# One product with the scalar features instead of two in the message pass of a four-layer graph network

## The chip, the cores and the metric

The kernel runs on one core of one Trainium2 chip. The metric is the device time of one execution in microseconds (us). Of the kernel before, three runs took 8483.14, 8487.90 and 8493.29 us; the median is 8487.9 us. A difference of about 0.2% (17 us) is what such runs can tell from none.

The engines have these names in the profile: PE is TensorE (matrix products), PEld its weight loads, DVE is VectorE, ACT is ScalarE, POOL is GpSimd (it issues the gathers), SP issues the plain DMAs. PSUM is the memory that PE writes; it has eight banks of 512 float32 per partition, `c.ps[:, bank, :]`.

## What is computed

The kernel computes four graph layers one after the other on 6250 nodes and 100,000 edges. The change is in the first, whose messages are, for each edge:

```python
h = jax.nn.silu(edge_scalars @ (fc_w1 / ...)) * SILU_NORM
w = h @ (fc_w2 / ...)
w0, w1, w2, w3 = the four quarters of w, 32 wide each
se = s[edge_src]          # 32 scalar features of the source node
ve = v[edge_src]          # 32 x 3 vector features
es = edge_attr[:, :1]
ev = edge_attr[:, 1:4]
mid_s0 = w0 * se * es
mid_s1 = w3 * jnp.einsum('eui,ei->eu', ve, ev) / SQRT3
mid_v0 = (w1 * se)[:, :, None] * ev[:, None, :]
mid_v1 = (w2 * es)[:, :, None] * ve
mid_scal = jnp.concatenate([mid_s0, mid_s1], axis=1)
mid_vec = jnp.concatenate([mid_v0, mid_v1], axis=1)
ns = jax.ops.segment_sum(mid_scal, edge_dst, num_segments=N) * inv
nv = jax.ops.segment_sum(mid_vec, edge_dst, num_segments=N) * inv
out_s = ns @ (w_lin2_s / fan)
```

So two of the four products have the scalar features `se` as a factor: one row of 32 with `w0`, three rows with `w1` times the three components of `ev`.

## The kernel before

The function `messages` holds this pass. The edges are sorted by destination and lie 128 to a chunk. There are 784 chunks, in 98 groups of 8 (`G8`, index `q`); a group has two halves of 4 chunks (`b` is 0 or 1). A ring of 4 groups (`RING`) holds gathered rows and loaded weights. Each engine has its own program; they meet at semaphores only, so what is written first on an engine runs first on it.

- **SP** (L930 to 962) loads the weights and attributes of a group (`s.pay4`, called `fld` in the trace), and stores finished rows.
- **POOL** (`gather`, L1149) issues one indirect DMA a chunk, which fetches the source rows of 128 edges into `rows`. It waits for the indices (ACT, L970) and, from the fifth group on, until the products of the group four places back are done (`m.prod`).
- **ACT** (`scaled`, L976 to 997) lays the weights of a half in PSUM, in banks 4 and 5 for `b` = 0 and 6 and 7 for `b` = 1. Two instructions copy `w0` and `w2` of the four chunks (L985), twelve copy `w1` and `w3` times one component of `ev` each (L989). It starts on a half when the products of the half two places back are done. In bank 4 lie the twelve rows of `w1`, then the four rows of `w0`; in bank 5 the same of `w3` and `w2`. Between halves it does steps of the node layer that runs behind (L1387 to L1407).
- **DVE** (L1016 to 1106) makes the one-hot places of a group (`hot`, L813 through `one_hot`), the products in five steps (`products`, L1031 to 1072), and adds what PE returns to `acc` (`add_item`, L824). The five steps are: 0, `w3` times the vector features into `s.dot`, which the trace calls `u` (L1056); 1, `w0` times the scalar features (L1060); 2, the three rows of `w1` times the scalar features (L1063); 3, `w2` times the vector features (L1067); 4, the sum of `s.dot` over the three components (L1071), with which `m.prod` is signalled.
- **PE** (L1103 to 1124) multiplies the one-hot places of a chunk with its products (L1118, 257 columns) into PSUM bank 0 or 1. It waits at each half for `m.prod`, and at each chunk until the sum two places back has been added (`ahead = 2`).

The order on DVE is written out in `reduce` (L1082 to 1099): step 0 of half 1; then for the four chunks of half 0 an add and a step each; then `hot` of the next group and step 0 of its half 0; then for the chunks of half 1 an add and a step of the next group's half 0 each. A step of the node layer (L1417 to L1430), or the add of the rows left over in a node tile (L857), stands in between in some groups.

The names: `plain_in` and `scaled_in` are the parts of the PSUM banks with the unscaled and the scaled weights, `s.prod4` is the output seen as chunk, four rows, 64 columns. `s.lin2` are the weights by which the summed messages are multiplied afterwards; their rows follow the column order of `prod4`.

Of the kernel before, what the change touches and what calls it, by code (L numbers as in the profile page):

```python
# [18 lines left out]
ALU = mybir.AluOpType  # L19
ACT = mybir.ActivationFunctionType  # L20
# [889 lines left out]
def messages(c, s, table, layer):  # L910
# [9 lines left out]
    rows_of = lambda r: ring_rows(c, r, D)  # L920
    ahead = 2
    bank = lambda q, j: item(q * G8 + j) % ahead
    scaled_in = lambda b, t, j: c.ps[:, 4 + 2 * b:6 + 2 * b, (j % 4) * 3 * MUL:(j % 4 + 1) * 3 * MUL] if t is None else \
        c.ps[:, 4 + 2 * b + t, 0:4 * 3 * MUL].rearrange("p (j a u) -> p j a u", j=4, a=3)
    plain_in = lambda b: c.ps[:, 4 + 2 * b:6 + 2 * b, 4 * 3 * MUL:4 * 4 * MUL].rearrange("p t (j u) -> p t j u", j=4)

    with nc.Block() as block:

# [36 lines left out]
        @block.scalar  # L965
        def _(act):
            def indices(i, r):
                q = RING * i + r
                act.wait_ge(m.pay[r].sem, i * 16 + (m.pay[r].n + 16))
                nc.scalar.activation(c.idx["dst"][:, at(q, G8, 0, G8)], s.pay4[:, r, :, SRC],  # L970
                                     ACT.Copy).then_inc(c.idx_ready.sem, 1)
                nc.scalar.activation(c.lo["dst"][:, at(q, G8, 0, G8)], s.pay4[:, r, :, LO],
                                     ACT.Copy).then_inc(m.kept.sem, 1)

            def scaled(i, r):
                q = RING * i + r  # L976

                act.wait_ge(m.pay[r].sem, i * 16 + (m.pay[r].n + 16))
                for j in range(G8):
                    if j % 4 == 0 and q:  # L980
                        act.wait_ge(m.prod.sem, m.prod.n + q * 2 + j // 4 - 1)
                    if j % 4 == 0:
                        w02 = s.pay4[:, r, j:j + 4, 0:P].rearrange("p j (t u) -> p t j u", t=4)[:, 0:4:2, :, :]
                        for t in range(2):
                            nc.scalar.activation(plain_in(j // 4)[:, t, :, :], w02[:, t, :, :], ACT.Copy)  # L985
                    w13 = s.pay4[:, r, j, 0:P].rearrange("p (t u) -> p t u", t=4)[:, 1:4:2, :]
                    for a in range(3):
                        to = scaled_in(j // 4, None, j)[:, :, a * MUL:(a + 1) * MUL]
                        last = nc.scalar.activation(to, w13, ACT.Copy,  # L989
                                                    scale=s.pay4[:, r, j, EV + a:EV + a + 1])  # L990
                    if j % 4 == 3:
                        last.then_inc(m.scaled.sem, 1)
                    if j == 3 and after(i, r, 3, RING):
                        indices(*after(i, r, 3, RING))
                    layer.act(act, q * G8 + j)
            lay_places(c, nc.scalar)
            indices(0, 0)
            indices(0, 1)
            indices(0, 2)
            written_out(NG, scaled, RING)  # L1000
            for t in range(NCH, NCH + layer.after):
                layer.act(act, t)
# [15 lines left out]
        def _(dve):  # L1018
# [14 lines left out]
            def products(i, r, b, step):  # L1033


                q = RING * i + r
                js = slice(4 * b, 4 * b + 4)
                w = plain_in(b)
                g = rows_of(r)[:, js, :].rearrange("p j (t u) -> p j t u", t=4)
                if step == 0:  # L1040
                    if b == 0:
                        dve.wait_ge(c.gathered[r].sem, i * (16 * G8) + (c.gathered[r].n + 16 * G8))
                    if q:

                        dve.wait_ge(c.mm.sem, c.mm.n + done(q * G8 + 4 * b - 4))
                        h = 2 * (q - 1) + b
                        if h < STASH:
                            sent = c.stashed[h % (2 * RING)]
                            dve.wait_ge(sent.sem, sent.n + 16 * (h // (2 * RING) + 1))

                    dve.wait_ge(m.scaled.sem, q * 2 + (m.scaled.n + b + 1))
                    if not (first(q) and b == 0):

                        dve.wait_ge(m.prod.sem, q * 2 + (m.prod.n + b))

                    nc.vector.tensor_tensor(s.dot, scaled_in(b, 1, 0), g[:, :, 1:4, :],  # L1056
                                            ALU.mult).then_inc(m.dotted.sem, 1)
                elif step == 1:

                    nc.vector.tensor_tensor(s.prod4[:, js, 0, MUL:2 * MUL], w[:, 0, :, :], g[:, :, 0, :], ALU.mult)  # L1060
                elif step == 2:

                    nc.vector.tensor_tensor(s.prod4[:, js, 1:4, 0:MUL], scaled_in(b, 0, 0),  # L1063
                                            g[:, :, 0:1, :].broadcast_to([P, 4, 3, MUL]), ALU.mult)
                elif step == 3:

                    nc.vector.tensor_tensor(s.prod4[:, js, 1:4, MUL:2 * MUL],  # L1067
                                            w[:, 1, :, :].unsqueeze(2).broadcast_to([P, 4, 3, MUL]), g[:, :, 1:4, :], ALU.mult)
                else:
                    dve.wait_ge(m.dotted.sem, q * 2 + (m.dotted.n + b + 1))  # L1070
                    nc.vector.tensor_reduce(s.prod4[:, js, 0, 0:MUL], s.dot.rearrange("p j a u -> p j u a"),  # L1071
                                            AX.X, ALU.add).then_inc(m.prod.sem, 1)

            def add(q, j, bin_):
# [24 lines left out]
                        products(*after(i, r, 1, RING), 0, j - 3)  # L1099
            wait_places(c, dve)  # L1100
            hot(0, 0)
            for step in range(5):
                products(0, 0, 0, step)  # L1103
            written_out(NG, reduce, RING)
            for t in range(NCH, NCH + layer.after):
# [1392 lines left out]
def prepare_weights(c, s):  # L2498
# [3 lines left out]
    with nc.Block() as block:  # L2502

        @block.sync
        def _(sp):

            sp.wait_ge(c.store.sem, c.store.n)

        @block.scalar
        def _(act):  # L2510

            act.wait_ge(c.load.sem, c.load.n)
            nc.scalar.activation(s.sig[:, :], s.sig[:, :], ACT.Exp, scale=-1.0).then_inc(s.m.rooted.sem, 1)

        @block.vector
        def _(dve):
            st = Steps(dve, c.dve)
            dve.wait_ge(c.load.sem, c.load.n)
            st(v.tensor_scalar(s.fc1[:, :], s.fc1[:, :], 8 ** -0.5, None, ALU.mult))
            st(v.tensor_scalar(s.fc2[:, :], s.fc2[:, :], SILU_NORM * 64 ** -0.5, None, ALU.mult))  # L2520

            scale = 0.25 * (2 * MUL) ** -0.5
            st(v.tensor_scalar(s.lin2[:, :], s.lin2[:, :], scale, None, ALU.mult)).wait()
            st(v.tensor_scalar(s.lin2[0:MUL, 0:MUL], s.lin2[0:MUL, 0:MUL], 3 ** -0.5, None, ALU.mult))
            heads = lambda ap: ap.rearrange("p (h u) -> p h u", h=HEADS)
            of = heads(s.wg[:, 0:D + HEADS])
            st(v.tensor_tensor(heads(s.attw[:, 0, :]), of[:, :, 0:CH], heads(s.att[:, 0, :]), ALU.mult))
            st(v.tensor_tensor(s.attw[:, 1, :], s.wdst[:, :], s.att[:, 1, :], ALU.mult)).wait()
            st(v.tensor_reduce(of[:, :, CH], heads(s.attw[:, 0, :]), AX.X, ALU.add))
            st(v.tensor_reduce(s.wg[:, D + HEADS:D + 2 * HEADS], heads(s.attw[:, 1, :]), AX.X, ALU.add))  # L2530
            st.wait()
            st(v.memset(s.attw[:, :, :], 0.0)).wait()
            st(v.tensor_copy(s.attw[:, 0, 0:MUL], s.lin2[:, 0:MUL]))
            for i, a in enumerate((0, 1, 1)):
                to = s.attw[:, a, MUL:D].rearrange("p (u i) -> p i u", i=3)[:, i, :]
                st(v.tensor_copy(to, s.lin2[:, (i + 1) * MUL:(i + 2) * MUL]))
            dve.wait_ge(s.m.rooted.sem, s.m.rooted.n + 1)
            st(v.tensor_scalar(s.sig[:, :], s.sig[:, :], 1.0, None, ALU.add)).wait()
            st(v.reciprocal(s.sig[:, :], s.sig[:, :])).wait()
            for l in range(3):  # L2540
                w, a = s.w[l][:, :], s.sig[:, l:l + 1]
                st(v.tensor_scalar(w, w, a, None, ALU.mult))
                st(v.tensor_scalar(s.b[l][:, :], s.b[l][:, :], a, None, ALU.mult))
# [7 lines left out]
def gnn(nc, A, out, upto=None):  # L2551
    with ExitStack() as ctx:
# [7 lines left out]
        def lay(width, dt=F32):  # L2560
# [129 lines left out]
        halves = lambda t: t[:, :].rearrange("p (a n) -> p a n", a=2)  # L2690
        s.first_weights = [(s.lin1[0:MUL, 0:MUL], A["L0_gnn_w_lin1_s"])]
        s.weights = [(s.fc1[:, :], A["L0_gnn_fc_w1"]), (s.fc2[:, :], A["L0_gnn_fc_w2"]),
                     (s.lin2[0:MUL, 0:MUL], A["L0_gnn_w_lin2_s"][MUL:2 * MUL, :]),
                     (s.lin2[MUL:2 * MUL, 0:MUL], A["L0_gnn_w_lin2_s"][0:MUL, :]),
                     (s.lin2[2 * MUL:P, MUL:2 * MUL], A["L0_gnn_w_lin2_v"]),
                     (s.lin2[0:2 * MUL, 2 * MUL:3 * MUL], A["L0_gnn_w_lin2_v"]),
                     (s.lin2[2 * MUL:P, 3 * MUL:4 * MUL], A["L0_gnn_w_lin2_v"]),
# [165 lines left out]
```

## Time and profile before

| | |
|---|---|
| Median of three runs | 8487.9 us |
| The profiled execution | 8494.57 us |
| Its span in the trace | 8492.8 us, mean granted TensorE clock 0.758 |
| DVE busy | 5705.7 us (67%) |
| PE busy | 5666.3 us (67%) |
| POOL busy | 6043.0 us (71%) |
| ACT busy | 3353.5 us (39%) |
| The message pass, first to last step 0 to 4 | from 1170.83 to 2225.15 us of the span |

The page puts no weight on one line in its chain of waits, so the reading goes by stage. The message pass is 1054 us, an eighth of the span. The pass after it gathers from a table that this one writes, so its gathers begin only when the message pass is over (the first at 2237.32 us), and time that is lost or gained in the pass moves all that follows.

### The profile page before, as it was taken

To read this page: it belongs to the slowest core of one execution; us is meant where nothing else is said; L and a number is where in the kernel's file an instruction comes from. 1 tells how busy PE (TensorE), PEld (TensorE's weight loads), DVE (VectorE), ACT (ScalarE), POOL (GpSimd) and SP (SyncE) were. 2 spreads that over 40 slices of the span, in tenths; PEclk is the share of its full clock that TensorE was granted. 3 is DMA by queue.
4 is the path that set the end of the run, shared out by engine and by line. 5 is a ranking of instruction groups with operands and counts; after the bars stand their busy time and mean duration, and the time that the engine had idled before them with its cause. 6 is when DMAs were issued, how large, how long until landed. Compare 5 with 4: busy or idle time off the path is not lost. (4 is left out here: it accounts for less than half of the span.)

```text
span 8492.8 us, 105913 instructions
## 1 busy us (share of the span) xinstructions
PE 5666.3 (67%) x23206; PEld 3954.1 (47%) x23206; DVE 5705.7 (67%) x15407; ACT 3353.5 (39%) x10636; POOL 6043.0 (71%) x6427
## 2 busy tenths in 40 slices
PE   5777747667666666676676776666655555788885
PEld 3444424444444444444444443444444444666664
DVE  8959148888666666666666666555544444788887
ACT  3333347777455553433323332000001111566665
POOL 2777767776577777777777776777777777666664
PEclk6555557777788888999989998888865555788886
DMA  2111144344222224444344444544433322111111
GB/s 75 59 58 59 58 120 113 111 112 111 77 64 64 63 63 128 119 119 119 111 146 119 119 118 133 122 116 116 116 89 62 62 62 60 50 49 49 49 49 38
DMA packets 632226, 749.12 MB, mean 88 GB/s; under 512 B 257061, under 2 KB 490169, under 8 KB 631465
## 3 DMA queue, kind: packets, MB, share of 16 engines
q0 software_dynamic: 239808, 572.66, 23.6%
q1 hardware_dynamic: 391512, 169.55, 7.9%
q8 instruction: 194, 3.18, 0.2%
q14 instruction: 440, 3.60, 0.1%
q10 hardware_dynamic: 272, 0.14, 0.0%
HBM read 617.05 MB, written 124.77 MB: 87 GB/s over the span
## 5 line engine op out<-in xcount | busy, mean ns | idle before, releaser
L824 DVE TENSOR_TENSOR acc<-acc,ps 128x256 f32 (+3 forms) x4704 | 1762.2, 375 | 1632.7 <-PE ps L1866 1245.6
L1149 POOL DMA_INDIRECT rows<-table_gcn,index_dst x1984 | 1890.1, 953 | 671.8 <-issue 574.6
L1866 PE MATMUL ps<-rows,hot 128*128 128x256 f32 (+2 forms) x5536 | 1517.4, 411 | 1229.9 <-DMA rows<-table_gcn,index_dst 495.4
L1866 PEld LDWEIGHTS ps<-rows,hot 128*128 128x128 f32 x5536 | 1110.2, 248 | 1631.0 <-issue 700.4
L1760 ACT ACTIVATE ut<-u,fld 128x128 f16<-128x128 f16 x1568 | 541.8, 392 | 1533.4 <-DVE u L1808 1532.8
L1149 POOL DMA_INDIRECT rows<-table_gat,index_dst x832 | 784.8, 943 | 375.3 <-issue 238.8
L1149 POOL DMA_INDIRECT rows<-table_lin,index_dst x784 | 739.8, 944 | 302.3 <-issue 231.9
L1149 POOL DMA_INDIRECT rows<-table_mean,index_src x784 | 741.2, 945 | 249.3 <-issue 230.2
L1118 PE MATMUL ps<-prod,hot 128*128 128x257 f32 x1568 | 635.6, 543 | 394.2 <-DVE prod L1071 313.3
L1851 PE MATMUL ps<-prod,ut 128*128 128x392 f16 x3136 | 738.3, 364 | 0.5 <-ACT ut L1760 0.5
L1149 POOL DMA_INDIRECT hot_v<-table_gcn,index_dst x576 | 547.9, 951 | 175.5 <-issue 166.7
L1149 POOL DMA_INDIRECT pay<-table_gcn,index_dst x576 | 547.6, 951 | 175.4 <-issue 164.2
L1118 PEld LDWEIGHTS ps<-prod,hot 128*128 128x128 f32 x1568 | 346.7, 257 | 645.4 <-issue 255.4
L989 ACT ACTIVATE ps<-fld 128x64 f32<-128x64 f32 x2352 | 577.2, 298 | 0.0
L692 POOL DMA_INDIRECT dst_rows<-pay,acc x398 | 384.6, 966 | 262.1 <-ACT pay L670 141.3
L1866 PE MATMUL ps<-pay,hot 128*128 128x256 f32 x1152 | 368.1, 454 | 236.9 <-DMA pay<-table_gcn,index_dst 154.9
L611 PEld LDWEIGHTS ps<-fc,prod 64*128 64x128 f32 x1564 | 340.6, 327 | 389.8 <-issue 364.0
L611 PE MATMUL ps<-fc,prod 64*128 64x128 f32 x1564 | 367.0, 426 | 230.9 <-ACT pay L670 116.6
L2242 ACT ACTIVATE hot_v<-prod,rows 128x128 f32<-128x128 f32 x1664 | 507.3, 387 | 4.6 <-DMA rows<-table_gat,index_dst 1.3
L1866 PE MATMUL ps<-hot_v,hot 128*128 128x256 f32 x1152 | 364.2, 450 | 213.5 <-DMA hot_v<-table_gcn,index_dst 135.1
L813 DVE TENSOR_TENSOR hot<-ps,place_dst 128x1024 f32<-128x1024 f32 x392 | 477.0, 1217 | 6.9 <-ACT ps L804 6.8
L2436 PE MATMUL ps<-ident,hot_v 128*128 128x128 f32 x1664 | 320.9, 325 | 200.2 <-DVE mx L2306 123.5
(429 smaller groups left out, 11086.0 us busy)
## 6 DMA issues: line engine op xcount, KB each, us to landing
fld<-dst_rows SPq DMA_DIRECT2D x98, 544.0 KB, 4.2
rows<-table_gcn,index_dst POOLq DMA_INDIRECT x1984
table_gcn<-acc SPq DMA_DIRECT2D x147, 128.0 KB
fld<-left_rows SPq DMA_DIRECT2D x147, 128.0 KB
pay<-dst_rows SPq DMA_DIRECT2D x832, 1.0 KB
rows<-table_gat,index_dst POOLq DMA_INDIRECT x832
rows<-table_lin,index_dst POOLq DMA_INDIRECT x784
rows<-table_mean,index_src POOLq DMA_INDIRECT x784
```

The costliest lines, as they stand in the source:

```text
L611: last = pe.matmul(c.ps[:, 2 + b, j * P:(j + 1) * P], hid[:, q % 2, b, j * P:(j + 1) * P], s.fc2[:, :], start=True, stop=True)
L692: pool.indirect_dma_start(s.dst_rows, bass.IndirectOffsetOnAxis(ap=s.pos_i[:, t:t + 1], axis=0), slot(q)[:, j, :], None).then_inc(m.sc[q % ...
L813: c.nc.vector.tensor_tensor(c.hot[:, h, :, :], c.ps[:, PLACES, 0:P].unsqueeze(1).broadcast_to([P, G8, P]), places.broadcast_to([P, G8, P]) ...
L824: c.nc.vector.tensor_tensor(to, to, product, ALU.add).then_inc(c.added.sem, 1)
L989: last = nc.scalar.activation(to, w13, ACT.Copy, scale=s.pay4[:, r, j, EV + a:EV + a + 1])
L1118: pe.matmul(c.ps[:, bank(q, j), 0:AU], c.hot[:, r % 2, j, :], s.prod[:, j, 0:AU], start=True, stop=True).then_inc(c.mm.sem, 1)
L1149: pool.indirect_dma_start(to(q, j), None, table, bass.IndirectOffsetOnAxis(ap=c.idx[k][:, t:t + 1], axis=0)).then_inc(c.gathered[q % per]. ...
L1760: last = nc.scalar.activation(s.row_val[:, z, i, :], s.row_hot[:, z, :], ACT.Copy, scale=s.columns[:, 2 + i, at(q, per, n0 + j, 1)])
L1851: last = pe.matmul(c.ps[:, 4 + b, 0:half], s.row_val[:, r, i, :], s.col_hot[:, r, b * half:(b + 1) * half], start=opens and i == 0, stop=e ...
L1866: pe.matmul(c.ps[:, bank(q, j), 0:used], c.hot[:, r % 2, j, :], row_of(c, s, r, j, used), start=True, stop=True).then_inc(c.mm.sem, 1)
L2242: last = nc.scalar.activation(s.hot_v[:, j, a, :], s.mask8[:, j, :], ACT.Identity, bias=rows[:, j, a, CH:HW], scale=NEG)
L2436: last = pe.transpose(c.ps[:, b % 2, k * P:(k + 1) * P], s.hot_v[:, 2 * b + k // 2, k % 2, :], c.ident[:, :])
```

## The change

ACT lays the weights of a half as four rows a chunk in each of its two banks: `w0`, then the three of `w1`; in the other `w2`, then the three of `w3`. It issues as many instructions as before; two of them now write four rows of 32 that lie 128 apart, where they wrote 128 in a row. With this the rows of `w0` and `w1` are next to each other, and DVE's steps 1 and 2 become one instruction, whose output is the first 32 columns of all four rows of `prod4`. Step 0 and the step with `w2` now read every fourth row or three rows of four, where they read one run. The sum over components goes to columns 32 to 63 of row 0, and `lin2` is laid out to match, with one load fewer at the start.

The products have four steps instead of five. The loops over chunks are unchanged, so the step with which `m.prod` is signalled now stands ahead of the last add of a half.

```diff
-    scaled_in = lambda b, t, j: c.ps[:, 4 + 2 * b:6 + 2 * b, (j % 4) * 3 * MUL:(j % 4 + 1) * 3 * MUL] if t is None else \
-        c.ps[:, 4 + 2 * b + t, 0:4 * 3 * MUL].rearrange("p (j a u) -> p j a u", j=4, a=3)
-    plain_in = lambda b: c.ps[:, 4 + 2 * b:6 + 2 * b, 4 * 3 * MUL:4 * 4 * MUL].rearrange("p t (j u) -> p t j u", j=4)
+    weights_in = lambda b: c.ps[:, 4 + 2 * b:6 + 2 * b, :].rearrange("p t (j a u) -> p t j a u", j=4, a=4)
+    scaled_in = lambda b, j, a: weights_in(b)[:, :, j % 4, a + 1, :]
+    plain_in = lambda b: weights_in(b)[:, :, :, 0, :]
...
-                        to = scaled_in(j // 4, None, j)[:, :, a * MUL:(a + 1) * MUL]
-                        last = nc.scalar.activation(to, w13, ACT.Copy,
+                        last = nc.scalar.activation(scaled_in(j // 4, j, a), w13, ACT.Copy,
...
-                w = plain_in(b)
+                w = weights_in(b)
...
-                    nc.vector.tensor_tensor(s.dot, scaled_in(b, 1, 0), g[:, :, 1:4, :],
+                    nc.vector.tensor_tensor(s.dot, w[:, 1, :, 1:4, :], g[:, :, 1:4, :],
                                             ALU.mult).then_inc(m.dotted.sem, 1)
                 elif step == 1:
 
-                    nc.vector.tensor_tensor(s.prod4[:, js, 0, MUL:2 * MUL], w[:, 0, :, :], g[:, :, 0, :], ALU.mult)
+                    nc.vector.tensor_tensor(s.prod4[:, js, :, 0:MUL], w[:, 0, :, :, :],
+                                            g[:, :, 0:1, :].broadcast_to([P, 4, 4, MUL]), ALU.mult)
                 elif step == 2:
 
-                    nc.vector.tensor_tensor(s.prod4[:, js, 1:4, 0:MUL], scaled_in(b, 0, 0),
-                                            g[:, :, 0:1, :].broadcast_to([P, 4, 3, MUL]), ALU.mult)
+                    nc.vector.tensor_tensor(s.prod4[:, js, 1:4, MUL:2 * MUL],
+                                            w[:, 1, :, 0:1, :].broadcast_to([P, 4, 3, MUL]), g[:, :, 1:4, :], ALU.mult)
                 elif step == 3:
-
-                    nc.vector.tensor_tensor(s.prod4[:, js, 1:4, MUL:2 * MUL],
-                                            w[:, 1, :, :].unsqueeze(2).broadcast_to([P, 4, 3, MUL]), g[:, :, 1:4, :], ALU.mult)
-                else:
                     dve.wait_ge(m.dotted.sem, q * 2 + (m.dotted.n + b + 1))
-                    nc.vector.tensor_reduce(s.prod4[:, js, 0, 0:MUL], s.dot.rearrange("p j a u -> p j u a"),
+                    nc.vector.tensor_reduce(s.prod4[:, js, 0, MUL:2 * MUL], s.dot.rearrange("p j a u -> p j u a"),
                                             AX.X, ALU.add).then_inc(m.prod.sem, 1)
...
-            for step in range(5):
+            for step in range(4):
                 products(0, 0, 0, step)
...
-            st(v.tensor_scalar(s.lin2[0:MUL, 0:MUL], s.lin2[0:MUL, 0:MUL], 3 ** -0.5, None, ALU.mult))
+            st(v.tensor_scalar(s.lin2[MUL:2 * MUL, 0:MUL], s.lin2[MUL:2 * MUL, 0:MUL], 3 ** -0.5, None, ALU.mult))
...
-                     (s.lin2[0:MUL, 0:MUL], A["L0_gnn_w_lin2_s"][MUL:2 * MUL, :]),
-                     (s.lin2[MUL:2 * MUL, 0:MUL], A["L0_gnn_w_lin2_s"][0:MUL, :]),
+                     (s.lin2[0:2 * MUL, 0:MUL], A["L0_gnn_w_lin2_s"]),
```

What stands in a row on DVE before, in the message pass, from the last adds of a group's half 1 to the first add of the next group (L793 loads the numbers of the bins; `u` is `s.dot`):

```order
L1063 TENSOR_TENSOR prod<-ps,rows 128x4x3x32
L824 ISA
L824 TENSOR_TENSOR acc<-acc,ps 128x257
L1067 TENSOR_TENSOR prod<-ps,rows 128x4x3x32
L824 ISA
L824 TENSOR_TENSOR acc<-acc,ps 128x257
L1071 TENSOR_REDUCE prod<-u 128x4x32
L793 TENSOR_LOAD bin_of_dst
L1056 TENSOR_TENSOR u<-ps,rows 128x384
L824 ISA
L824 TENSOR_TENSOR acc<-acc,ps 128x257
L1060 TENSOR_TENSOR prod<-ps,rows 128x4x32
```

The same place on DVE in the changed kernel, whose line numbers are lower by 1 to 4 (L1059 is the joined product, L1067 the sum over components):

```order
L1059 TENSOR_TENSOR prod<-ps,rows 128x4x4x32
L824 ISA
L824 TENSOR_TENSOR acc<-acc,ps 128x257
L1063 TENSOR_TENSOR prod<-ps,rows 128x4x3x32
L824 ISA
L824 TENSOR_TENSOR acc<-acc,ps 128x257
L1067 TENSOR_REDUCE prod<-u 128x4x32
L824 ISA
L824 TENSOR_TENSOR acc<-acc,ps 128x257
L793 TENSOR_LOAD bin_of_dst
L1055 TENSOR_TENSOR u<-ps,rows 128x384
L824 ISA
```

The sum over components moved ahead of the last add of the half, and one product is gone from the row. The same holds at the other half, where `hot` (L813) stands in place of L793. PE, POOL and SP have the same rows in the same order as before.

## Rows read from the trace of the kernel before

**Rows 1.** Stretches: us, busy PE, PEld, DVE, ACT, POOL, clock, DMA share, GB/s
```profile
1171.00:1315.00 144.00, 94.23 (x246) 53.45 (x246) 122.45 (x284) 98.55 (x422) 108.94 (x116) 0.73 0.56 159
1315.00:2215.00 900.00, 625.66 (x1769) 381.94 (x1768) 760.71 (x1887) 655.84 (x2843) 622.09 (x660) 0.73 0.39 108
...
1621.50:1627.00 5.50, 3.63 (x8) 2.17 (x8) 4.28 (x11) 4.11 (x18) 4.13 (x5) 0.69 0.65 185
...
1602.00:1606.50 4.50, 2.44 (x8) 1.27 (x8) 4.12 (x11) 3.85 (x17) 3.28 (x5) 1.00 0.73 212
```

**Rows 2.** Waits, 1160 to 2230 us: waiting engine <- awaited: us, times, longest us
```profile
ACT ps L985 <- DVE prod L1071: 197.2, 132, 4.9
...
DVE acc L824 <- PE ps L1118: 107.7, 239, 3.0
...
POOL rows L1149 <- DVE prod L1071: 40.9, 26, 3.3
POOL rows L1149 <- ACT index_dst L970: 29.5, 22, 8.7
...
DVE u L1056 <- ACT ps L989: 6.8, 15, 0.7
```

**Rows 3.** Timeline (start us, duration us): first and last gather, two starts of a group
```profile
1159.48 0.99 POOL L1149 DMA_INDIRECT rows<-table_lin,index_dst  x1 [8.71 <-ACT index_dst L970]
...
1315.07 0.55 DVE L1056 TENSOR_TENSOR u<-ps,rows 128x384 f32<-128x384 f32 x1
...
2191.89 0.94 POOL L1149 DMA_INDIRECT rows<-table_lin,index_dst  x1 [0.30 <-issue]
...
2214.70 0.54 DVE L1056 TENSOR_TENSOR u<-ps,rows 128x384 f32<-128x384 f32 x1
```

**Rows 4.** Timeline of DVE, one group from `hot` to `hot`, at mixed clock
```profile
1617.38 1.21 DVE L813 TENSOR_TENSOR hot<-ps,fld 128x1024 f32<-128x1024 f32 x1
...
1618.98 0.41 DVE L824 TENSOR_TENSOR acc<-acc,ps 128x257 f32 x1
1619.31 0.28 DVE L1060 TENSOR_TENSOR prod<-ps,rows 128x128 f32<-128x128 f32 x1
1619.60 0.42 DVE L824 TENSOR_TENSOR acc<-acc,ps 128x257 f32 x1
1619.94 0.55 DVE L1063 TENSOR_TENSOR prod<-ps,rows 128x384 f32<-128x384 f32 x1
1620.41 0.41 DVE L824 TENSOR_TENSOR acc<-acc,ps 128x257 f32 x1
...
1621.53 0.58 DVE L1071 TENSOR_REDUCE prod<-u 128x128 f32<-128x384 f32 x1
1622.25 0.56 DVE L1056 TENSOR_TENSOR u<-ps,rows 128x384 f32<-128x384 f32 x1
1623.56 0.42 DVE L824 TENSOR_TENSOR acc<-acc,ps 128x257 f32 x1 [0.75 <-PE ps L1118]
...
1625.41 0.42 DVE L824 TENSOR_TENSOR acc<-acc,ps 128x257 f32 x1
...
1626.55 0.58 DVE L1071 TENSOR_REDUCE prod<-u 128x128 f32<-128x384 f32 x1
1627.05 1.21 DVE L813 TENSOR_TENSOR hot<-ps,fld 128x1024 f32<-128x1024 f32 x1
```

**Rows 5.** Timeline of DVE, another group at full granted clock, both its ends
```profile
1597.82 1.21 DVE L813 TENSOR_TENSOR hot<-ps,fld 128x1024 f32<-128x1024 f32 x1
...
1606.54 1.22 DVE L813 TENSOR_TENSOR hot<-ps,fld 128x1024 f32<-128x1024 f32 x1
```

**Rows 6.** Groups of instructions by line: busy us, mean ns of one, idle before
```profile
L1063 DVE TENSOR_TENSOR prod<-ps,rows 128x384 f32<-128x384 f32 x196 | 107.8, 550 | 0.0
L1067 DVE TENSOR_TENSOR prod<-ps,rows 128x384 f32<-128x384 f32 x196 | 107.7, 550 | 0.0
L985 ACT ACTIVATE ps<-fld 128x128 f32<-128x128 f32 x392 | 92.9, 269 | 197.6 <-DVE prod L1071 197.2
```

## The prediction

> **What bounds the kernel now.** The kernel is a string of passes with a hard end between them, so I read the message pass alone: first the busy time by stretch, then the waits of the pass, then the timeline at the two ends and inside two groups. In the stretches [rows 1] the reader is to compare POOL's count. Until 1315 us it issues 116 gathers in 144 us, one every 1.24 us, which is a gather's 0.94 us and the 0.30 us behind it [rows 3]: it never stops. A group of 8 costs it 9.97 us, and DVE, which has no node layer to serve yet, keeps that pace. From 1315 to 2215 us there are 660 gathers in 900 us, one in 1.36 us. There POOL waits, 40.9 us for DVE's last step and, of its 29.5 us for indices, all but the first 8.7 us [rows 2], because the ring of four groups is full. The two starts of a group show DVE's own pace: 1315.07 us is group 14's, 2214.70 us group 97's [rows 3], so 83 groups took 899.6 us, **10.84 us each**. From group 14 on DVE's program is the bound, with PE in its loop: DVE is busy 760.7 of 900 us, and most of the rest is its 107.7 us of waiting for PE's sums in the pass (239 times) [rows 2]. Before group 14 the gathers are the bound and nothing that DVE saves counts.
>
> **The cap.** From the first gather, 1159.48 us, 783 intervals of 1.245 us (0.94 or 0.95 and 0.30) and one gather give 2135.3 us as the earliest end of the last; it ended at 2192.8 us. That is 57 us. DVE stood 21.9 us behind the last gather when it began the last group (2214.70 less 2192.83). Where the gathers lead, it stands 2 to 6 us behind: the first step 0 came at 1170.83 us (the table above) with the eighth gather over near 1169.2, and group 14 began at 1315.07 with the 120th over near 1309.1 us (119 intervals on). I take 4, so 18 us more can come back: **the pass can give 75 us and no more**.
>
> **The change part by part.** Steps 1 and 2 become one. On DVE an instruction's price is the distance to the next start. A product of 128 elements gives way after 0.29 us, one of 384 after 0.47 us [rows 4]. The joined one has 512 elements, which the trace does not show; the durations 0.28 and 0.55 us are 1.04 ns an element apart, so I take 0.55 + 0.13 = 0.68 us long and 0.60 us to the next start. That saves 0.16 us a half, **0.33 us a group**. Its bounds are 0.47 us (as short as 384 elements) and 0.76 us (the sum of the two).
>
> The step that signals `m.prod` moves ahead of the last add of the half. In the group at mixed clock, add to add and half to half [rows 4]: from the first add of half 1 (1618.98) to the first add of the next half 0 (1623.56) it is 4.58 us. The end of it is a chain through PE: the sum over components starts at 1621.53, then PE multiplies, and the add can start 2.03 us later; DVE has only the loading of the bins and step 0 to do in that time (step 0 starts 0.72 us after the sum, the add could follow 0.47 us after that), and idles 0.75 us. Now an add stands in the gap. New length: add to joined product 0.33, to the add 0.60, to the `w2` product 0.34, to the add 0.47, to the sum 0.33, which is 2.07; then the longer of DVE's own 0.50 + 0.72 + 0.47 = 1.69 and PE's 2.03. Together 4.10 us, 0.48 us less. The other half, from 1623.56 to `hot` at 1627.05, takes 3.49 us. Two adds that use the same bank are at least 1.85 us apart here (1623.56 to 1625.41), since PE has to multiply in between; DVE's own 0.34 + 0.60 + 0.34 + 0.47 = 1.75 us stays under that, so the third add comes at 1.85 us. The second comes at 0.94, the fourth not before 0.94 + 1.85 = 2.79, and `hot` 0.33 later at 3.12 us: 0.37 us less. **At mixed clock a group saves 0.85 us**, 9.67 to 8.82 us.
>
> At full clock the group takes 8.72 us from 1597.82 to 1606.54 [rows 5], at a granted clock of 1.00 against 0.69 in the lower half of the other one [rows 1]. There PE's chain is short and DVE's own work decides: `hot` to the first add 1.60 (1617.38 to 1618.98), then 2.07 and 1.69, then 0.34 + 0.60 + 0.34 + 0.47 + 0.33 + 0.50 + 0.33 = 2.91. Together 8.27 us: **at full clock 0.45 us**. The mean granted clock of the pass is 0.73 [rows 1], lower than that of either group, so the lower-clock price should be the common one; but in some groups a step of the node layer or a left-over add already fills the time in which DVE would wait, and its saving is nearer 0.45. I take 0.80 us a group: 83 x 0.80 = 66 us.
>
> What hides it or takes it back. **ACT**: the number and width of its instructions are the same, and it writes every row of 32 in one piece as L989 does now; I take nothing for it. DVE waits for ACT's weights 15 times, 6.8 us in all [rows 2]; in those halves ACT, which stood waiting for PE in its node-layer step, is last, and the 0.4 us that a half saves is not got. That is 15 x 0.4 = 6 us off. The rest of ACT's slack stays: it starts on a half when the sum two halves back is done, and step 0 comes one add later behind that sum than before, which makes up for the shorter half. It also sat 197.2 us waiting for DVE [rows 2]. **POOL**: its waits go, since 10.84 less 0.72 is 10.12 us a group, still a little over 9.97. **Reading rows that lie apart**: the `w2` product already reads each row of 32 three times over, in 550 ns, the same as the one that reads 384 in a run [rows 6]; so step 0 and this one stay at 0.55 us. **The start**: one load fewer and a scaling on other partitions, outside the pass and off any path, nothing.
>
> Sum: 66 - 6 = **60 us**. The profiled execution took 8494.6 us, 1.8 us more than its span, and the median of the runs is 6.7 us lower. 8494.6 - 60 - 6.7 = 8427.9, say **8428 us**.
>
> **The rivals.**
>
> *The gathers become the bound.* If DVE saves over 10.84 - 9.97 = 0.87 us a group, POOL never waits and the pass gives its cap. For it: at mixed clock I have 0.85 us, at half clock throughout more. It also comes out if PE's granted clock rises: at full clock a plain group takes 8.27 us, and even with the 1.2 us by which the mean group before (10.84) exceeds the plain one at mixed clock (9.67) that is under 9.97. Time: 8488 - 75 = 8413 us. The Trainium skill, "TensorE: Matmul & The Clock Gate", Part 1, says that the clock follows how busy the engine has lately been, so that PE with fewer waits might be granted more; whether it does here no row shows, for 0.73 stood in both stretches although POOL's pace differed [rows 1].
>
> *Only one of the two gains comes.* Either PE's chain does not shorten, because the add that is pulled into the gap was itself what PE's bank waited for; then 0.33 x 83 = 27 us are left, 8461 us. Or the joined product costs as much as the two (the change does not do what it says): then 60 - 27 = 33 us, 8455 us. Against the first stands that PE idles before the first product of half 0 until the sum is done; against the second the even 1.04 ns an element.
>
> *ACT takes the place of the saved time.* Its two plain copies a half, 269 ns each [rows 6], now write four rows 512 bytes apart. If each became 0.2 us longer, 0.8 us a group would be added to ACT's loop; with halves where its slack is already nil, the pace would stay near 10.8 us: 8480 to 8490 us, no difference.
>
> *Slower: PSUM rows that lie apart are read at half rate.* Step 0 and the `w2` product would each take 0.40 us more (384 elements at 1.04 ns), 1.6 us a group against 0.8 saved. 83 x 0.8 = 66 us more and some 10 us in the first 14 groups, which then no longer keep up with the gathers: about 8564 us. It turns from gain to loss where the two together lose more than 0.40 us a half. Against it: L1067 with its repeated rows is as fast as L1063 [rows 6]; but its rows, though repeated, lie next to each other. The Trainium skill, "PSUM — Partial Sum Buffer", Specifications, speaks against the change in the same way: it gives cache lines of 8 bytes and says that a pattern that is not contiguous slows matmuls significantly. It says so of matmuls, and the rows here are 128 bytes and more in one piece, so it changes this rival's chance little.
>
> **How the numbers follow.** The forecast (a gain of 45 to 70 us) has 0.50, the gathers as bound 0.19, one gain only 0.15, no difference 0.10, slower 0.06. The range from 8411 to 8466 us holds the first three, 0.84. Faster by over 0.2% (below 8471 us, which is about what a measurement of this kernel can tell) is 0.84; within 0.2% 0.10; slower 0.06.
>
> **What would show it.** In the changed profile: 196 joined products of 0.68 us with 0.60 us to the next start; step 0 and the `w2` product at 0.55 us; ACT's plain copies at 0.27 us. DVE's wait for PE's sums falls from 107.7 to under 60 us. Groups from 14 on take 10.0 to 10.2 us, the last gather ends between 2136 and 2150 us, and DVE stands behind it less than before. POOL's 40.9 us of waiting for the last step nearly go. I am wrong if a step has grown, if the groups stay over 10.5 us, or if the time comes back after the pass, whose next gather should start about 12 us after the last sum as it does now.

## The result and the profile after

The changed kernel takes 8416.6 us (median of five runs, 8413.9 to 8423.0) against 8491.2 us for the kernel before beside it. The ratio is 0.9911, with a 95% interval from 0.9899 to 0.9922: **75 us or 0.9% faster**. The forecast was 8428 us, a gain of 60; the case called "the gathers become the bound" had 8413 us.

These views show where the time went. First the stretch that begins at 1315 us, as in [rows 1]; it ends where the gathers now end: us, busy PE, PEld, DVE, ACT, POOL with counts, granted clock, DMA share, GB/s.

```profile
1315.00:2137.00 822.00, 560.72 (x1755) 317.90 (x1756) 722.23 (x1707) 644.23 (x2814) 621.18 (x659) 0.86 0.43 118
```

From 1315 us on, 660 gathers took 900 us before; now 659 take 822, one every 1.25 us to the end. And the granted clock of this stretch is 0.86, where it was 0.73. The waits of the pass (1160 to 2150 us), as in [rows 2]:

```profile
ACT ps L985 <- DVE prod L1067: 86.5, 63, 4.2
...
DVE u L1055 <- DMA rows<-table_lin,index_dst: 50.3, 43, 10.9
...
DVE acc L824 <- PE ps L1114: 23.3, 46, 2.1
...
DVE u L1055 <- ACT ps L988: 13.5, 24, 1.0
...
POOL rows L1145 <- ACT index_dst L970: 8.9, 1, 8.9
...
POOL rows L1145 <- DVE prod L1067: 4.0, 13, 0.3
```

DVE's wait for PE's sums fell from 107.7 us and 239 times to 23.3 us and 46 times. In its place stands a wait for gathered rows, 43 times. In the kernel before that wait was this (1160 to 2230 us):

```profile
DVE u L1056 <- DMA rows<-table_lin,index_dst: 14.9, 3, 10.9
```

So the bound has changed hands. POOL hardly waits for anybody after the start: its 13 entries for DVE are at most 0.3 us each, no more than the gap that stands behind every gather. The timeline of the last gather, of step 0 of the last group's two halves, and of the last sum over components:

```profile
2136.78 0.94 POOL L1145 DMA_INDIRECT rows<-table_lin,index_dst  x1 [0.30 <-issue]
...
2139.38 0.55 DVE L1055 TENSOR_TENSOR u<-ps,rows 128x384 f32<-128x384 f32 x1
...
2144.07 0.56 DVE L1055 TENSOR_TENSOR u<-ps,rows 128x384 f32<-128x384 f32 x1 [0.34 <-PE ps L1114]
...
2147.32 0.58 DVE L1067 TENSOR_REDUCE prod<-u 128x128 f32<-128x384 f32 x1
```

The last gather ends at 2137.72 us, 55.1 us earlier than before [rows 3], and the pass at 2147.90 us, 10.2 us behind it, where it was 32.3 us behind. The pass is 77 us shorter and the span 71.6 us. 1.5 us of the difference lie right behind the pass: the first gather of the next one starts 13.7 us after the last sum (2161.59 us), where it started 12.2 us after it.

Inside a group that has neither a node-layer step nor a left-over add, DVE's timeline reads now, at mixed clock (compare [rows 4]):

```profile
1569.73 1.22 DVE L813 TENSOR_TENSOR hot<-ps,fld 128x1024 f32<-128x1024 f32 x1
...
1571.33 0.41 DVE L824 TENSOR_TENSOR acc<-acc,ps 128x257 f32 x1
1571.66 0.68 DVE L1059 TENSOR_TENSOR prod<-ps,rows 128x512 f32<-128x512 f32 x1
1572.26 0.41 DVE L824 TENSOR_TENSOR acc<-acc,ps 128x257 f32 x1
...
1573.38 0.58 DVE L1067 TENSOR_REDUCE prod<-u 128x128 f32<-128x384 f32 x1
1573.88 0.41 DVE L824 TENSOR_TENSOR acc<-acc,ps 128x257 f32 x1
1574.44 0.56 DVE L1055 TENSOR_TENSOR u<-ps,rows 128x384 f32<-128x384 f32 x1
1575.21 0.42 DVE L824 TENSOR_TENSOR acc<-acc,ps 128x257 f32 x1 [0.21 <-PE ps L1114]
...
1578.32 1.22 DVE L813 TENSOR_TENSOR hot<-ps,fld 128x1024 f32<-128x1024 f32 x1
```

It takes 8.59 us where the one before took 9.67. The add stands between the sum and step 0 (1573.88), and of the 0.75 us that DVE idled before the next add 0.21 are left.

### The profile page after: what moved, and what is told of

Its sections match the earlier page's. It is cut to its first block and busy times, and to the rows that moved or that the text cites. A ratio compares the mean times of both kernels' runs of the same rounds, so it can differ in the third digit from the quotient of the medians.

```text
span 8421.2 us, 105716 instructions
## 1 busy us (share of the span) xinstructions
PE 5596.3 (66%) x23206; PEld 3877.0 (46%) x23206; DVE 5678.2 (67%) x15211; ACT 3349.2 (40%) x10636; POOL 6042.4 (72%) x6427
## 5 line engine op out<-in xcount | busy, mean ns | idle before, releaser
L1114 PE MATMUL ps<-prod,hot 128*128 128x257 f32 x1568 | 592.1, 494 | 365.6 <-DVE acc L824 197.2
L1114 PEld LDWEIGHTS ps<-prod,hot 128*128 128x128 f32 x1568 | 299.1, 227 | 625.8 <-DVE acc L824 350.2
L813 DVE TENSOR_TENSOR hot<-ps,place_dst 128x1024 f32<-128x1024 f32 x392 | 477.2, 1217 | 7.3 <-ACT ps L804 7.2
```

Source lines behind the costliest of these rows:

```text
L813: c.nc.vector.tensor_tensor(c.hot[:, h, :, :], c.ps[:, PLACES, 0:P].unsqueeze(1).broadcast_to([P, G8, P]), places.broadcast_to([P, G8, P]) ...
L1114: pe.matmul(c.ps[:, bank(q, j), 0:AU], c.hot[:, r % 2, j, :], s.prod[:, j, 0:AU], start=True, stop=True).then_inc(c.mm.sem, 1)
```

## The experiments

Each run stands beside runs of the kernel before on the same chip; their medians were 8492.3 us (first four), 8491.0 (next four) and 8495.3 us (last four).

**The theory** was that two things act, and not equally: the sum over components, and with it the signal to PE, comes one add earlier, which takes an idle time out of a loop through PE; and one product's fixed cost is gone. The rival was that the shorter work on DVE is the gain. A second question was whether the gathers cap it.

### The joined product alone

```diff
+            def products(i, r, b, slot):
+                for step in ((0,), (1,), (2,), (), (3,))[slot]:
+                    product_step(i, r, b, step)
...
+            for slot in range(5):
+                products(0, 0, 0, slot)
```

> The changed kernel with the sum over components put back behind the last add of the half: the joined product alone. The third place between adds, now free, stays empty, so two adds stand next to each other. If the gain is the earlier signal to PE, little is left: at lower clock the two adds that share a bank stay 1.85 us apart and nothing is saved, at full clock 0.33 us a group, so a gain of 5 to 27 us, 8464 to 8486 us, and DVE still waits some 100 us for PE's sums. If the gain is the shorter work of DVE, as much as 8430 us.

Measured: 8487.2 us, ratio 0.9991 (0.9982 to 1.0000). That is 5 us, and the interval reaches from 15 us to nothing. DVE's wait for PE in the pass (us, times, longest):

```profile
DVE acc L824 <- PE ps L1118: 109.2, 194, 2.4
```

That DVE has 0.33 us a group less to do turned into nothing that can be told for sure: it waits for PE as long as before. Since a place between two adds had to stay empty, I moved it in a second run.

```diff
-                for step in ((0,), (1,), (2,), (), (3,))[slot]:
+                for step in ((0,), (), (1,), (2,), (3,))[slot]:
```

> The joined product with the sum over components behind the last add as in the kernel before, the place that is free being between the first two adds of a half and not between the last two. If the run with the other free place gained nothing because of where its two adds stood together, this one gains 15 to 30 us (8460 to 8475 us). If it is the late signal that keeps the gain away: 8478 to 8492 us again.

Measured: 8500.6 us, ratio 1.0004 (0.9995 to 1.0013). No gain again (the run lies even over the 8478 to 8492 us expected of it, beside 8495.3 us for the kernel before), so it is not where the two adds stand together. What a run of this kind can't avoid is that two adds do stand together somewhere; that the late signal alone is at fault is shown only together with the next run.

### The earlier sum alone

The kernel before, its layout and both products, these two between the same adds:

```diff
+            def products(i, r, b, slot):
+                for step in ((0,), (1, 2), (3,), (4,), ())[slot]:
+                    product_step(i, r, b, step)
```

> The kernel before with its layout and its two separate products, but both between the same two adds, so that the sum over components comes ahead of the last add: the move alone. If the move is what counts, DVE keeps only 0.14 us a group more work than the changed kernel, the gathers are nearly the bound, and the time is 8420 to 8435 us, with DVE's wait for PE's sums under 50 us. If joining is what counts, it stays above 8460 us.

Measured: 8422.3 us, ratio 0.9916 (0.9902 to 0.9929), 70 us faster. **The move alone gives nearly all of it**, as far as the gathers let either kernel go; the changed kernel's interval (0.9899 to 0.9922) overlaps this one's. The waits say the same:

```profile
DVE u L1056 <- DMA rows<-table_lin,index_dst: 31.7, 27, 10.9
DVE acc L824 <- PE ps L1122: 31.1, 52, 2.1
```

### The layout alone

The new layout with five steps in the old places, `w0` and `w1` apart:

```diff
-                    nc.vector.tensor_tensor(s.prod4[:, js, :, 0:MUL], w[:, 0, :, :, :],
-                                            g[:, :, 0:1, :].broadcast_to([P, 4, 4, MUL]), ALU.mult)
+                    nc.vector.tensor_tensor(s.prod4[:, js, 0, 0:MUL], w[:, 0, :, 0, :], g[:, :, 0, :], ALU.mult)
+                elif step == 2:
+
+                    nc.vector.tensor_tensor(s.prod4[:, js, 1:4, 0:MUL], w[:, 0, :, 1:4, :],
+                                            g[:, :, 0:1, :].broadcast_to([P, 4, 3, MUL]), ALU.mult)
```

> The new layout in PSUM with five steps and the old places: rows that lie apart are written by ScalarE and read by VectorE, nothing is joined or moved. If the layout is free: 8491 us within 10, products at 0.55 us, ScalarE's copies at 0.27 us. If reading rows that lie apart costs something that the gain of the change covered up: over 8510 us.

Measured: 8493.6 us, ratio 1.0005 (0.9996 to 1.0014). The groups of instructions (busy us, mean ns of one):

```profile
L1062 DVE TENSOR_TENSOR prod<-ps,rows 128x384 f32<-128x384 f32 x195 | 107.4, 551 | 0.0
L1066 DVE TENSOR_TENSOR prod<-ps,rows 128x384 f32<-128x384 f32 x195 | 107.3, 551 | 0.0
L1059 DVE TENSOR_TENSOR prod<-ps,rows 128x128 f32<-128x128 f32 x195 | 55.3, 284 | 0.0
...
L985 ACT ACTIVATE ps<-fld 128x128 f32<-128x128 f32 x392 | 92.8, 269 | 184.8 <-DVE prod L1070 183.9
```

All three products and ACT's copies are as long as before to within 1 ns, and so is step 0, whose mean is 552 ns in both. The slower rival, PSUM rows read at half rate, and the rival in which ACT takes the time back, are both gone.

### Are the gathers the bound?

The changed kernel without the product with `w2`, whose part of the messages is missing:

> The changed kernel without the product with w2 (that part of the messages is left out): VectorE has 0.94 us a group less to do. If the gathers are the bound of the changed kernel's pass, hardly anything comes of it: 8405 to 8417 us, the last gather still ends near 2137 us and VectorE waits longer for gathered rows. If VectorE is still the bound: 8325 to 8345 us.

```diff
                 elif step == 2:
-
-                    nc.vector.tensor_tensor(s.prod4[:, js, 1:4, MUL:2 * MUL],
-                                            w[:, 1, :, 0:1, :].broadcast_to([P, 4, 3, MUL]), g[:, :, 1:4, :], ALU.mult)
+                    pass
```

Measured: 8421.8 us, ratio 0.9916 (0.9901 to 0.9931). An instruction of 0.55 us less in each half, and no gain at all (5 us over the range expected of it with the gathers as bound). DVE waits instead, longer for PE and for gathered rows both:

```profile
DVE acc L824 <- PE ps L1112: 62.7, 122, 2.1
DVE u L1055 <- DMA rows<-table_lin,index_dst: 61.4, 52, 10.9
```

The other way round, four kernels with half of the gathers left out from the fifth group on. Half of their chunks then use rows of an earlier group, so their output is wrong and only their time counts:

```diff
+            for q in range(NG):
+                ready(q)
+                for j in range(G8 if q < RING else 4):
+                    t = q * G8 + j
+                    pool.indirect_dma_start(rows_of(q % RING)[:, j, :], None, table,
```

> The kernel before with half of the gathers of the message pass left out from the fifth group on (the products then use older rows in four of eight chunks), so that GpSimd can't be the bound. VectorE was it already from group 14 on: 10.7 to 10.8 us a group, 8475 to 8491 us.

> The changed kernel with the same half of the gathers left out: VectorE's own pace without the cap. If the gathers hide part of what the change saves: 9.5 to 9.7 us a group, the pass 25 to 45 us shorter than in the changed kernel, 8372 to 8392 us. If 9.97 us a group is VectorE's own pace too: 8410 to 8417 us.

> The joined product alone (sum over components after the last add of the half) with half of the gathers left out. By the theory of the earlier signal: 0 to 30 us under the kernel before with half of the gathers. By the theory of shorter work: near the changed kernel with half of the gathers.

> The earlier sum over components alone, products apart, with half of the gathers left out. By the theory of the earlier signal: 10 to 20 us over the changed kernel with half of the gathers, and most of the way from the kernel before. By the theory of shorter work: near the kernel before with half of the gathers.

| Half of the gathers left out | us | ratio to before (95%) | clock, 1315 to 2050 us |
|---|---|---|---|
| kernel before | 8496.9 | 1.0006 (0.9997 to 1.0016) | 0.77 |
| joined product, late sum | 8485.7 | 0.9993 (0.9983 to 1.0002) | 0.80 |
| apart, early sum | 8389.6 | 0.9881 (0.9865 to 0.9898) | 0.86 |
| changed kernel | 8379.8 | 0.9872 (0.9855 to 0.9888) | 0.88 |

The kernel before gains nothing from half the gathers (it lies 6 us over the range expected of it); the changed one gains 37 us. So the gathers hid that much of the change, and **without them it is worth 117 us**: 107 for the move, and 10 or 11 for the join with either place of the sum. The intervals of the ratios overlap in both pairs that differ by the join alone. But with the early sum the four runs with the join (8373.2 to 8382.0 us) all lie below the four without it (8386.8 to 8393.0), so that it gives something is clear; its size is not.

The 117 us are 1.19 us for each of 98 groups, but not evenly. With half of the gathers, group 14 begins at 1319.14 us in the kernel before and at 1300.12 us in the changed one, which is 19 us in the first 14 groups. From there to group 97 (2210.00 and 2096.16 us) a group takes 10.73 and 9.59 us: 1.14 us less. The stretch from 1315 to 2050 us of the kernel before in this form:

```profile
1315.00:2050.00 735.00, 501.89 (x1467) 306.67 (x1466) 627.80 (x1558) 542.82 (x2356) 258.10 (x274) 0.77 0.32 86
```

and of the changed one, in which PE has 1637 matmul entries where it had 1467 (a product of a chunk makes two entries, and the node layer's are among them):

```profile
1315.00:2050.00 735.00, 510.51 (x1637) 289.64 (x1636) 669.96 (x1592) 601.15 (x2630) 288.59 (x306) 0.88 0.36 97
```

### What the clock does

1.14 us is more than two single groups show at like clock (below: 0.65 and 1.08 us), and the clock had risen. In this stretch, 1315 to 2050 us, it was 0.74 to 0.80 in the six profiles with the late sum and 0.84 to 0.88 in the six with the early one. To see whether it is a cause, I left DVE's order as before and gave PE something to do in the time in which it waits for the sum over components: two products of the constant identity a half, into the free bank that the next real product overwrites.

```diff
-                    if j % 4 == 0:
-                        pe.wait_ge(m.prod.sem, q * 2 + (m.prod.n + j // 4 + 1))
                     if item(q * G8 + j) >= ahead:
                         pe.wait_ge(c.added.sem, c.added.n + item(q * G8 + j) - ahead + 1)
+                    if j % 4 == 0:
+                        for _ in range(2):
+                            pe.matmul(c.ps[:, bank(q, j), 0:P], c.ident[:, :], c.ident[:, :], start=True, stop=True)
+                        pe.wait_ge(m.prod.sem, q * 2 + (m.prod.n + j // 4 + 1))
```

> The kernel before with two products of the constant identity (128 columns) on PE at the start of each half, into a bank that is free, in the time in which PE waits for the sum over components; nothing else differs. If it is PE's granted clock that part of the gain comes from, and the clock follows how busy PE is: the clock of the pass rises from 0.73 over 0.80, DVE's wait for PE's sums falls from 107.7 us, and the time is 8440 to 8480 us. If the clock plays no part or does not follow: 8488 to 8510 us.

Measured: 8425.3 us, ratio 0.9916 (0.9902 to 0.9929). **Work that computes nothing gives 70 us**, more than was expected if the clock plays a part (8440 to 8480 us), and as much as the change within the intervals. The stretch and the waits of this kernel:

```profile
1315.00:2050.00 735.00, 532.62 (x2153) 331.24 (x2154) 662.95 (x1669) 579.88 (x2516) 555.70 (x589) 0.96 0.45 119
```

```profile
DVE acc L824 <- PE ps L1120: 36.6, 93, 2.9
...
DVE u L1056 <- DMA rows<-table_lin,index_dst: 28.3, 23, 11.0
```

The granted clock is 0.96 (2.4 GHz nearly throughout) where the same stretch of the kernel before has 0.74, the wait for PE's sums a third of what it was, and the gathers are the bound here too (589 gathers in 735 us, one in 1.25 us). The timeline of PE shows why it costs nothing: the products of the identity (L1118, the first row) are over before the sum that the real ones (L1120) wait for.

```profile
1600.00 0.71 PE L1118 MATMUL ps<-ident 128*128 128x128 f32 x4
1601.30 0.70 PE L1120 MATMUL ps<-prod,hot 128*128 128x257 f32 x2 [0.58 <-DVE prod L1071]
```

Does the fill-in work through the clock, or does it also make the product behind it start or end sooner? The timelines of DVE settle it. From the start of the sum over components to the add of the first product behind it, the kernel before needs 1.50 us where the clock is 1.00:

```profile
1601.97 0.58 DVE L1071 TENSOR_REDUCE prod<-u 128x128 f32<-128x384 f32 x1
1602.69 0.56 DVE L1056 TENSOR_TENSOR u<-ps,rows 128x384 f32<-128x384 f32 x1
1603.47 0.42 DVE L824 TENSOR_TENSOR acc<-acc,ps 128x257 f32 x1 [0.23 <-PE ps L1118]
```

and 2.03 us in the group of [rows 4], where the clock is 0.50 while PE works in between (from 1622.22 us on). With the fill-in it is 1.48 us, at 1.00:

```profile
1606.95 0.58 DVE L1071 TENSOR_REDUCE prod<-u 128x128 f32<-128x384 f32 x1
...
1608.43 0.42 DVE L824 TENSOR_TENSOR acc<-acc,ps 128x257 f32 x1 [0.21 <-PE ps L1120]
```

So a chain at full clock is as long as it was, and there are more of them. Of the 62 places from 1315 us to the end of the pass where only step 0 stands between the sum and the add, 18 took 1.6 us or less in the kernel before and 41 took 1.95 us or more; with the fill-in it is 48 and 7.

The Trainium skill, "TensorE: Matmul & The Clock Gate", Part 1, says that the clock follows how busy PE has been; this run agrees, 0.96 against 0.74 in the same stretch. The same fill-in in the changed kernel with half of the gathers left out:

> The changed kernel with half of the gathers left out and the two products of the identity on PE per half. The clock of the pass is 0.87 without them. If a higher clock is worth something beyond the change: 9.3 to 9.5 us a group and 8355 to 8375 us, against 8379.8 us. If the fill-in products get in the way of the real ones, 8385 us or more.

Measured: 8361.8 us, ratio 0.9845 (0.9830 to 0.9860), 18 us under the 8379.8 us without it (23 us by the two ratios, since the kernel before beside it was slower by 4 us; their intervals touch), at a clock of 0.95:

```profile
1315.00:2050.00 735.00, 553.03 (x2291) 347.64 (x2291) 677.62 (x1621) 610.58 (x2675) 294.20 (x312) 0.95 0.37 99
```

So the higher clock is worth at least 70 us to the old order, which then meets the gathers, and some 20 us to the new one. In the new one DVE had only 24.8 us of waiting for PE's sums left, 46 times, before the fill-in.

### What is left at the gathers' bound

The changed kernel with a semaphore for each half of a group's gathers:

```diff
-                    if b == 0:
-                        dve.wait_ge(c.gathered[r].sem, i * (16 * G8) + (c.gathered[r].n + 16 * G8))
+                    landed = c.gathered[2 * r + b]
+                    dve.wait_ge(landed.sem, i * (16 * 4) + (landed.n + 16 * 4))
...
-                                    ).then_inc(c.gathered[q % per].sem, 16)
+                                            ).then_inc(c.gathered[2 * (q % RING) + j // 4].sem, 16)
```

> The changed kernel with a semaphore for each half group of gathers, so that step 0 of half 0 waits for four gathers and not for eight. With the gathers as bound the pass ends as far behind the last gather as DVE needs: it now ends 10.2 us behind it, then about 5 us, 8408 to 8414 us. If DVE were the bound, nothing: 8416 us.

Measured: 8412.7 us, ratio 0.9901 (0.9885 to 0.9916). This is the lowest time of a kernel here that computes all that the changed one does, but its interval overlaps the changed kernel's: faster than before is shown, faster than the change is not. The trace shows the mechanism. The last gather ends at 2141.80 us and the last sum 5.5 us behind it, where it was 10.2 us:

```profile
2140.85 0.95 POOL L1013 DMA_INDIRECT rows<-table_lin,index_dst  x1 [0.30 <-issue]
...
2146.76 0.59 DVE L1073 TENSOR_REDUCE prod<-u 128x128 f32<-128x384 f32 x1
```

Not all of that is won in this profile. Its first gather starts 2.2 us later than the changed kernel's (1161.44 and 1159.20 us) and its last ends 4.1 us later, so from the first gather to the last sum it is 985.9 us against 988.7.

## Why the prediction was right, and where it was off

**The cap was right, the bound behind it was not the one forecast.** The forecast had DVE stay the bound at 10.12 us a group, just over the gathers' 9.97, and the gathers as bound were a rival with 0.19. The runs show the gathers as the bound: a group takes 9.99 us from group 14 to group 97 (1310.59 to 2139.38 us), and an instruction less on DVE gave nothing. The cap was worked out well: the gathers allowed 75 us; the pass gave 77 and the median 75. Both of its parts came back: the last gather ends 55.1 us earlier (57 forecast), and the last group begins 1.7 us behind it (2139.38 us) instead of 21.9, 20 us less (18 forecast).

It is the cap that kept the time in the forecast range. Without it the change is worth 117 us, which would be about 8374 us, far below the range's 8411. That the gain forecast by the sum, 60 us, lies near the measured 75 owes more to this limit than to the price of a group.

**The first 14 groups** gave a little: group 14 begins at 1310.59 us, 4.5 us earlier. The prediction called the gathers the bound there. The kernel before with half of the gathers begins group 14 at 1319.14 us, no earlier than 1315.07, so DVE's loop held that pace as well as the gathers did.

**The joined product** lasts 683 ns in the mean of 196 and gives way after 0.60 us (1571.66 to 1572.26), as worked out. The bounds at the price of 384 elements and of both products are out.

**What the join is worth** was overstated as a part of the sum: 0.33 us a group would be 27 us by itself. Alone it gave 5 us and none in the two runs, and 10 or 11 us where the gathers are no bound. The step that counted was the other one, and the prediction's own working said so for the lower clock (two adds that share a bank stay 1.85 us apart), yet kept "one gain only, 27 us" as a case. By that working the join would show at full clock, and in the two runs the clock was 0.78 and 0.76 from 1315 to 2050 us; no run here has the late sum and the join at full clock, so this stays an argument.

**The saving a group, 0.80 us, was the mis-sized term**, and it made the forecast 60 and not 75. Uncapped it measured 1.14 us from group 14 on. Two pieces are known. First, the group at full clock was to take 8.27 us and takes 8.07:

```profile
1721.68 1.22 DVE L813 TENSOR_TENSOR hot<-ps,fld 128x1024 f32<-128x1024 f32 x1
...
1725.83 0.41 DVE L824 TENSOR_TENSOR acc<-acc,ps 128x257 f32 x1
1726.39 0.56 DVE L1055 TENSOR_TENSOR u<-ps,rows 128x384 f32<-128x384 f32 x1
...
1729.75 1.22 DVE L813 TENSOR_TENSOR hot<-ps,fld 128x1024 f32<-128x1024 f32 x1
```

I had step 0 start 0.72 us behind the add, since it starts that long behind the sum before; it starts 0.56 us behind it. A distance from start to start can't be carried over from the sum to the add, since the sum lasts 0.58 us and the add 0.41: in both groups step 0 starts 0.13 to 0.15 us after the end of what stands ahead of the loading of the bins. The mixed-clock group came out 0.23 us under its 8.82 as well, nearly all of it between the first add of one half and that of the next (3.88 us instead of 4.10).

Second, the clock: I took 0.73 as given and weighed a higher one only as a rival. It rose to 0.86 with the earlier sum, and a chain from the sum to the add that takes 2.03 us at the lower clock takes 1.50 us at the higher. Why it rose is argued, not shown. The fill-in shows that more work on PE raises it. In the changed kernel PE's busy share from 1315 us on is 68% where it was 70%, but its entries come closer together, 2.13 for each us where it was 1.97. How the 1.14 us divides between the shorter chain and the clock is not settled; at like clock two single groups give 0.65 us (8.72 to 8.07, clock 1.00) and 1.08 us (9.67 to 8.59, mixed, 0.82 and 0.80 over the group). A small change of the clock need not show in the time: the layout alone stood at 0.78 where the kernel before stood at 0.74, with no gain.

**ACT and POOL**: ACT made DVE wait 24 times, 13.5 us, where 15 times and 6.8 us were assumed to stay: a small loss, hidden by the cap. POOL's waits went as said, 40.9 to 4.0 us.

**The rivals.** The gathers as bound (0.19) is what happened, and its 8413 us lies nearer to the 8416.6 measured than the forecast; it deserved more, since its condition, 0.87 us a group, lay beside my own 0.85 for the mixed group. Its other condition, a higher clock, came with the earlier sum in every run that had it. Of "only one of the two gains comes", the half in which the join alone stays is out, for the move stayed. The slower rival was tested and is out, and ACT's copies did not grow. That the next gather would start about 12 us after the last sum was off by 1.5 us (13.7).

## What to carry to other kernels

In a loop of several engines, count where the signal to the next engine stands before counting instructions: here moving it one add ahead gave 70 us (107 without the cap), removing 196 instructions gave 5, which is hardly told from nothing (10 or 11 without the cap). Work out the cap of the next bound first, from its own cadence, since it set the size of the gain here. And look at the granted clock of the stretch as something that the change can move: in this loop PE, which waited in every round, did its own work at a lower clock for it, as the fill-in showed.

## What the runs showed of the hardware that I had not expected

- Two products of a constant a half, in time that PE idled, raised the granted clock of the stretch from 0.74 to 0.96 (1315 to 2050 us) and took 70 us off a kernel whose other engines did exactly the same work (8495.3 to 8425.3 us).
- VectorE and ScalarE read and write PSUM rows of 32 float32 that lie 512 bytes apart as fast as one run: 551 against 550 ns for 384 elements, 269 and 269 ns for ScalarE's copy of 128.
- With the loading of a group's eight bin numbers between them, step 0 starts 0.13 to 0.15 us after the end of the instruction ahead of it, be that the sum (0.72 us after its start) or the add (0.56 us). Without a load in between, the next instruction starts some 0.08 us before the end of the one ahead, so the loading costs some 0.22 us in either place. But in nine groups of the changed kernel in which instructions of the node layer or of the left-over rows stand between the sum and the add, step 0 starts 0.08 or 0.09 us before the end of the add, and the loading costs nothing that shows. Why it hides there is open.
